# Expert stage: row loads wait for the group six back, filling rows sent in four lots

## The chip, the core and the metric

One Trainium2 chip, of which one core is used. The metric is device microseconds of one execution, the median of three runs. The core has five engines that run their own instruction streams and meet at semaphores: PE (matmul; its weight loads are the rows of PEld), DVE, ACT, POOL and SP. SP only issues transfers here. POOL issues the indirect transfers, in which every row of a tile goes to an address of its own.

## What is computed

The whole program is two transformer-like layers; the change touches only the last part of the second, a mixture of experts over 8 x 512 tokens of width 256 with 16 experts, each token going to its best two:

```
router_logits = sigmoid(x @ gate_w + gate_b)
expert_values, expert_indices = top_k(router_logits, k=2)
expert_values = expert_values / sum(expert_values)
hg = x @ experts_wg[e];  hu = x @ experts_wu[e]      # 256 -> 128, per expert
out_e = (silu(hg) * hu) @ experts_wd[e]              # 128 -> 256
return x + shared_mlp(x) + sum_k expert_values[k] * out_e[k]
```

## The kernel before

The stage ahead of this one writes a row for each (token, expert) pair into a scratch tensor in HBM, `rows_dram`, sorted by expert: 512 16-bit words of the token (a high and a low part of 256 values), the row of the result that it is for, and its gate value. Each expert has a region of its own there. The expert stage (`expert_stage`, from L1973) then works through 80 tiles of 128 rows: 64 full tiles, whose places and experts are known only at run time, and 16 last tiles, one for each expert, of which only a part is filled. So that a last tile can be read whole, 128 *filling rows* are scattered behind the rows of each expert (L2016), 16 indirect transfers by POOL; they point at spare rows of the result.

Four tiles make a group: `G=4`, `NG=20` groups, of which `NF=16` (groups 0 to 15) hold full tiles and 16 to 19 the last tiles. Each group goes through this pipeline:

- SP loads its four tiles into one of six buffers, `xt[:,g%XB]`, `XB=6` (L1997 to L1999). It first reads the address of each tile (L1998). For g >= 6 it first waits (L1996) on the semaphore of a scatter, and for g == 16 on all filling rows (L1995).
- PE transposes the four tiles, 16 transposes, "turn" (L2024 to L2029); ACT and DVE copy them out of PSUM (L2068, L2091).
- PE multiplies by the gate and up weights, 48 matmuls, `upward` (L2046). The expert of a full tile is a register value, so the address of its weights is computed by PE's sequencer in between. For groups 16 to 19 it is a constant.
- ACT takes silu (L2079), DVE multiplies (L2102), ACT and DVE split the product into two 16-bit parts (L2082, L2104).
- PE multiplies by the down weights, 12 matmuls, `downward` (L2054); ACT and DVE scale by the gate value into one of four output buffers, `yt[:,g%YB]`, `YB=4` (L2072, L2095).
- POOL scatters the four output tiles to `found_dram` (L2020), reading the target rows from the group's `xt` buffer. That is why an `xt` buffer is free only when its group is scattered. There are four scatter semaphores, `scattered[g%YB]`.

In PE's order the turn of group g+1 stands ahead of `upward(g)`, and `downward(g-1)` behind it. So PE runs turn(g+1), upward(g), downward(g-1), turn(g+2) and so on; a turn that waits holds up the matmuls of the groups before it. On ACT and DVE the order is: copy of the turned g+1, work on g, output of g-1.

POOL's order is: 16 transfers of filling rows, then the scatters of groups 0 to 19. When all scatters have landed (L2000) SP reads the results back in eight pieces, DVE adds the two results of a token and the base, and SP stores the output (L2001 to L2012).

Of the kernel before, what the change touches and what calls it, by code (L numbers as in the profile page):

```python
# [34 lines left out]
@contextmanager  # L35
def semaphores(nc, stage):

    taken=[]
    def take(name):
        taken.append(nc.alloc_semaphore(name=stage+name))  # L40
        return taken[-1]
    yield take
    nc.clear_and_free_semaphores(taken)
    nc.all_engine_barrier()
# [1928 lines left out]
def expert_stage(nc, XT, HT, ident, wall, tile_row, last_row, group_experts, pad, pad_row, rows_dram, found_dram, out):  # L1973

    NT=NB*T//P; REGION=NB*T+P; FULL=2*NT; MAXT=FULL+NE; ROW=D+2; I32=mybir.dt.int32
    base=HT[:,:,:,:].rearrange("p k b t -> p (k b t)").rearrange("p (j d) -> p j d",d=D)
    room=XT[:,:,:,:].rearrange("p k b t -> p (k b t)")
    with ExitStack() as c2:
        sb2=lambda n,s,d=F32: c2.enter_context(nc.sbuf_tensor("exp_"+n,s,d))
        sem2=c2.enter_context(semaphores(nc,"exp_"))  # L1980
        G=4; NG=MAXT//G; NF=FULL//G; NC=NT//G; XB=6; YB=4
        ps=lambda n,s,d=F32: c2.enter_context(nc.psum_tensor("exp_"+n,s,d))
        px=[ps(f"turned{i}",[P,2,4,P],F16) for i in range(2)]; ph=[ps(f"hg{i}",[P,512]) for i in range(2)]; pu=[ps(f"hu{i}",[P,512]) for i in range(2)]; pd=[ps(f"out{i}",[P,2,D]) for i in range(2)]
        identh=sb2("identh",[P,P],F16)
        xt=sb2("xt",[P,XB,G,ROW],I32); xT=sb2("xT",[P,2,G,4,P],F16); si=sb2("silu",[P,2,512]); tg=sb2("tg",[P,2,512]); hid=sb2("hid",[P,2,2,512],F16)
        ob=sb2("ob",[P,2,G,D])
        found=room[:,0:4*G*D].rearrange("p (u c j d) -> p u c j d",u=2,c=2,d=D); yt=room[:,4*G*D:(4+YB)*G*D].rearrange("p (u j d) -> p u j d",u=YB,d=D)
        idh=sem2("identh"); loaded=[sem2(f"loaded{i}") for i in range(XB)]; turned=sem2("turned"); xt_kept=[sem2(f"turned_kept{i}") for i in range(2)]; up_done=sem2("up_done"); silu=sem2("silu"); product=sem2("product"); hi=sem2("hi"); lo=sem2("lo"); down=sem2("down"); y_kept=[sem2(f"y_kept{i}") for i in range(2)]; scattered=[sem2(f"scattered{i}") for i in range(YB)]
        pads_sent=sem2("pads_sent"); back=[sem2(f"back{i}") for i in range(2)]; paired=sem2("paired"); summed=sem2("summed"); stored=[sem2(f"stored{i}") for i in range(2)]
        block=c2.enter_context(nc.Block())  # L1990
        def words(g,d): return xt[:,g%XB].bitcast(d)
        @block.sync
        def _(sp):
            for g in range(NG):
                if g==NF: sp.wait_ge(pads_sent,16*NE)  # L1995
                if g>=XB: sp.wait_ge(scattered[g%YB],16*G*((g-XB)//YB+1))  # L1996
                for i in range(G):  # L1997
                    r=sp.value_load(tile_row[g*G+i:g*G+i+1,0:1] if g<NF else last_row[0:1,(g-NF)*G+i:(g-NF)*G+i+1],min_val=0,max_val=NE*(REGION+P)-P)  # L1998
                    sp.dma_start(xt[:,g%XB,i],rows_dram[bass.ds(r,P),:]).then_inc(loaded[g%XB],16)  # L1999
            for i in range(YB): sp.wait_ge(scattered[i],16*MAXT//YB)  # L2000
            def store(m):  # L2001
                sp.wait_ge(summed,m+1)
                for b in range(NB):
                    sp.dma_start(out[b,m*G*C:(m+1)*G*C,:].rearrange("(j t) d -> t j d",t=C),ob[b*C:(b+1)*C,m%2]).then_inc(stored[m%2],16)  # L2004
            for m in range(NC):
                if m>=2: sp.wait_ge(paired,m-1)
                for c in range(2):
                    at=c*NB*T+m*G*P
                    sp.dma_start(found[:,m%2,c],found_dram[at:at+G*P,:].rearrange("(j q) d -> q j d",q=P)).then_inc(back[m%2],16)
                if m: store(m-1)  # L2010
            store(NC-1)
            for i in range(2): sp.wait_ge(stored[i],16*NB*NC//2)  # L2012
        @block.gpsimd
        def _(pool):
            for e in range(NE):
                nc.gpsimd.indirect_dma_start(rows_dram[:,:],bass.IndirectOffsetOnAxis(pad_row[:,e:e+1],0),pad[:,e,:],None).then_inc(pads_sent,16)  # L2016
            for g in range(NG):
                for i in range(G):
                    if i%2==0: pool.wait_ge(y_kept[i//2],g+1)
                    nc.gpsimd.indirect_dma_start(found_dram[:,:],bass.IndirectOffsetOnAxis(words(g,U32)[:,i,D:D+1],0),yt[:,g%YB,i],None).then_inc(scattered[g%YB],16)  # L2020
# [158 lines left out]
def build(nc, a, out):  # L2179

    with ExitStack() as ctx:
# [39 lines left out]
        pad=sb("pad_rows",[P,NE,D+2],mybir.dt.int32); pad_row=sb("pad_row",[P,NE],U32)  # L2221
        rnn_dispatch_stage(nc,XT,HT,a["L1_cond2_Wx"],a["L1_cond2_Wh"],a["L1_cond2_b"],h0T,*[a["L1_ffn_"+n] for n in ("gate_w","gate_b","shared_wg","shared_wu","shared_wd","experts_wg","experts_wu","experts_wd")],ident,wall,tile_row,last_row,group_experts,pad,pad_row,rows_dram)
        expert_stage(nc,XT,HT,ident,wall,tile_row,last_row,group_experts,pad,pad_row,rows_dram,found_dram,out)


# [36 lines left out]
```

## Time and profile before

| | us |
|---|---|
| median of three runs | 3835.32 (3834.57 to 3835.72) |
| the profiled execution | 3842.36 |
| its span, first to last instruction | 3840.4 |
| expert stage, first load issued to last scatter issued | 3565.1 to 3783.8 |
| reading back and adding | 3785.4 to 3840.4 |

All times of the rows are from the start of the span, in us. A row of a timeline is one instruction, or some of one kind run together: start, duration, engine, line, operation, what it writes and reads, and in brackets how long its engine was idle before it and what ended that. Indirect transfers show only the time that POOL takes to issue them. In the chain of waits a row "DMA x<-y" is the time from issue until the data had landed. The ends of matmuls are modelled.

### The profile page before, as it was taken

The numbers are of one execution on the slowest core, as the hardware profiler recorded it, in microseconds if no ns is written. First come the engines' busy times: TensorE is split into PE (matmuls) and PEld (weight loads), VectorE is DVE, ScalarE is ACT, GpSimd is POOL, SyncE is SP. The second block draws the span as 40 slices with busy tenths as digits, with TensorE's granted clock in tenths as the row PEclk, the third lists the DMA queues.
The fourth block names the chain that finished last, engine by engine and source line by source line (L and its number), as shares of the span: only waits on it lengthen the run. The fifth ranks groups of instructions, "written<-read, shape, count | busy, mean of one in ns | idle before, by whom it ended". The sixth has DMA issues, their size and how long they took to land. (4 is left out here: it accounts for less than half of the span.)

```text
span 3840.4 us, 143685 instructions
## 1 busy us (share of the span) xinstructions
PE 3163.6 (82%) x58952; PEld 2402.2 (63%) x58952; DVE 2258.7 (59%) x6772; ACT 1695.6 (44%) x5164; POOL 1211.7 (32%) x1528
## 2 busy tenths in 40 slices
PE   8677488988889888489985899999999889999571
PEld 5445188888888888445532566666666567777451
DVE  4667644444444444368865888889888845555232
ACT  2179333333333333257743555565555534444230
POOL 0032410000000000033310655565555544444332
PEclk9899755555555555589997999999999955555786
DMA  4011100000000000010001000000000010110336
GB/s 132 1 55 46 31 25 14 25 14 14 25 14 25 14 14 25 13 34 21 20 1 52 2 3 3 2 3 3 2 3 2 16 50 31 33 33 28 109 97 173
DMA packets 112984, 116.09 MB, mean 30 GB/s; under 512 B 55041, under 2 KB 96458, under 8 KB 112371
## 3 DMA queue, kind: packets, MB, share of 16 engines
q1 hardware_dynamic: 104674, 87.36, 8.0%
q0 software_dynamic: 7824, 21.46, 1.5%
q8 instruction: 403, 6.60, 0.7%
q14 instruction: 83, 0.67, 0.1%
HBM read 79.65 MB, written 29.13 MB: 28 GB/s over the span
## 5 line engine op out<-in xcount | busy, mean ns | idle before, releaser
L676 PE MATMUL banks<-hp,whp 128*128 128x8 f16 x24576 | 741.4, 168 | 118.3 <-DVE hp L743 118.3
L676 PEld LDWEIGHTS banks<-hp,whp 128*128 128x128 f16 x24576 | 697.7, 104 | 179.1 <-DVE hp L743 170.2
L709 ACT ACTIVATE ig<-banks 128x32 f32<-128x32 f32 x512 | 101.4, 198 | 576.8 <-PE banks L676 576.8
L738 DVE SCALAR_TENSOR_TENSOR carry<-ig 128x16 f32<-128x16 f32 x512 | 92.1, 180 | 425.4 <-ACT ig L709 425.4
L646 POOL COPY HT<-hist 128x128 f32 x64 | 21.3, 408 | 987.0 <-DVE hp L748 987.0
L1747 PE MATMUL rnn_banks<-rnn_hp,rnn_whp 128*128 128x8 f16 x6144 | 285.6, 171 | 41.1 <-ACT rnn_hp L1805 15.6
L1747 PEld LDWEIGHTS rnn_banks<-rnn_hp,rnn_whp 128*128 128x128 f16 x6144 | 247.8, 107 | 108.3 <-ACT rnn_hp L1805 76.6
L1088 ACT ACTIVATE att_PH<-att_stp 128x1024 f16<-128x1024 f32 (+3 forms) x258 | 183.4, 711 | 296.6 <-PE att_stp L888 296.6
L1147 POOL TENSOR_TENSOR att_QK<-att_rot,att_QK 128x512 f16<-128x512 f32 x133 | 187.4, 1409 | 244.1 <-ACT att_QK L1080 244.1
L654 PE MATMUL banks<-xs,wxp 128*128 128x64 f16 x3168 | 263.7, 241 | 0.0
L1007 DVE TENSOR_TENSOR att_PL<-att_P,att_PH 128x1024 f16<-128x1024 f32 (+3 forms) x257 | 236.0, 957 | 0.5 <-issue 0.2
L1899 DVE TENSOR_TENSOR rnn_hp<-rnn_hist,rnn_hp 128x16 f16<-128x16 f32 x512 | 97.9, 191 | 228.7 <-ACT rnn_hist L1806 214.6
L1805 ACT ACTIVATE rnn_hp<-rnn_banks 128x16 f16<-128x16 f32 x512 | 94.3, 184 | 280.5 <-PE rnn_banks L1747 278.4
L832 PE MATMUL att_pj<-att_hT,att_w 128*128 128x512 f16 x804 | 199.2, 384 | 17.2 <-POOL att_hT L1151 15.4
L1138 POOL TENSOR_TENSOR att_ab<-att_ab,att_rope 128x512 f32<-128x512 f32 x134 | 170.0, 1269 | 131.7 <-DVE att_ab L980 128.7
L990 DVE TENSOR_REDUCE att_mx<-att_sp 128x2 f32<-128x264 f32 (+3 forms) x263 | 209.9, 820 | 1.1 <-PE att_sp L862 1.1
L654 PEld LDWEIGHTS banks<-xs,wxp 128*128 128x128 f16 x3168 | 194.6, 126 | 0.0
L1142 POOL TENSOR_TENSOR att_rot<-att_ab 128x512 f32<-128x512 f32 x134 | 185.6, 1385 | 15.3 <-POOL att_ab L1138 1.0
L901 PE MATMUL att_acc<-att_V,att_PH 128*128 128x65 f16 (+1 forms) x3584 | 181.1, 193 | 3.4 <-DVE att_PL L1010 3.4
L1093 ACT ACTIVATE att_P<-att_stp 128x1024 f32<-128x1024 f32 (+3 forms) x258 | 180.4, 699 | 5.3 <-DVE att_PL L1007 5.3
L901 PE MATMUL att_acc<-att_V,att_PL 128*128 128x65 f16 x1792 | 175.8, 192 | 0.0
L743 DVE TENSOR_TENSOR hp<-og,tc 128x16 f16<-128x16 f32 x512 | 90.2, 176 | 144.8 <-ACT tc L715 144.8
(595 smaller groups left out, 7767.1 us busy)
## 6 DMA issues: line engine op xcount, KB each, us to landing
gen_w<-in_L_cond_W_dram SPq DMA_DIRECT2D x32, 512.0 KB
exp_xt<-expert_rows_scratch SPq DMA_DIRECT2D x80, 129.0 KB
edge_cb<-cols_scratch SPq DMA_DIRECT2D x16, 512.0 KB, 3.7
XT<-expert_found_scratch SPq DMA_DIRECT2D x16, 512.0 KB, 5.0
mod_xn<-in_x_dram SPq DMA_DIRECT2D x8, 512.0 KB
XT<-in_xT_dram SPq DMA_DIRECT2D x1, 4096.0 KB
out_dram<-exp_ob SPq DMA_DIRECT2D x64, 64.0 KB, 2.2
attw_st<-in_L_attn_w_qkvT_dram SPq DMA_DIRECT2D x6, 512.0 KB
```

What stands on the lines that cost most here:

```text
L654: last=nc.tensor.matmul(out, wxp[:,wpart,k,col:col+128], xs[:,st,xpart,k,steps], start=False,stop=False,skip_group_check=True)
L676: last=nc.tensor.matmul(out, whp[:,wpart,k,col:col+128], hp[:,k,hpart], start=False,stop=True,skip_group_check=True)
L832: last=nc.tensor.matmul(pj[:,:],c_.w_of(n)[:,wpart,k,col:col+P],h_of(n)[:,xpart,k,PM:PM+T],start=(i==0),stop=(i==5)); i+=1
L901: last=nc.tensor.matmul(out[:,0:wide],p[:,h,at:at+P],V[:,n%4,tt,part,h,0:wide],start=(tt==0 and a==0 and p is PH and part==0),stop=(tt==(R ...
L990: i=nc.vector.tensor_reduce(out=mx[:,:,qt:qt+1],in_=s_ps[:,:,at:at+w_],axis=X_AX,op=ALU.max); at+=w_
L1007: i=nc.vector.tensor_tensor(PL[:,:,at:at+w_],P32[:,t%2,:,0:w_],PH[:,:,at:at+w_],ALU.subtract)
L1088: nc.scalar.activation(PH[:,:,at:at+w_],st_ps[:,:,0:w_],ACT.Exp,scale=DH**-0.5)
L1093: i=nc.scalar.activation(P32[:,t%2,:,0:w_],st_ps[:,:,0:w_],ACT.Exp,scale=DH**-0.5)
L1138: nc.gpsimd.tensor_tensor(ab[:,1],ab[:,1],c_.tab[:,1],ALU.mult).then_inc(turned,1)
L1142: nc.gpsimd.tensor_tensor(rot_of(j),ab[:,0],ab[:,1],ALU.add).then_inc(summed,1)
L1147: nc.gpsimd.tensor_tensor(dst[:,1],rot_of(j),dst[:,0],ALU.subtract).then_inc(lo,1)
L1747: last=nc.tensor.matmul(pre(st,par)[:,u,j], whp[:,wpart,k,u*P:u*P+P], hp[:,k,hpart], start=False,stop=True,skip_group_check=True)
```

## The change

Two edits in `expert_stage`.

1. The wait ahead of the load of group g (g >= 6) names the semaphore of group g-6, whose buffer is taken. Before, it named the semaphore with the number g%4 with the count for g-6. In effect, group 6 waited for group 2, 7 for 3, 8 and 9 for nothing more, 10 for 6, 11 for 7, 14 for 10, 15 for 11, 18 for 14 and 19 for 15. After, group g waits for g-6, throughout.
2. The filling rows are sent in `PG=4` lots of four transfers, ahead of the scatters of groups 0, 1, 2 and 3. Each lot first waits until group g+1 is turned.

```
-        G=4; NG=MAXT//G; NF=FULL//G; NC=NT//G; XB=6; YB=4
+        G=4; PG=4; NG=MAXT//G; NF=FULL//G; NC=NT//G; XB=6; YB=4
...
                 if g==NF: sp.wait_ge(pads_sent,16*NE)
-                if g>=XB: sp.wait_ge(scattered[g%YB],16*G*((g-XB)//YB+1))
+                if g>=XB: sp.wait_ge(scattered[(g-XB)%YB],16*G*((g-XB)//YB+1))
...
         @block.gpsimd
         def _(pool):
-            for e in range(NE):
-                nc.gpsimd.indirect_dma_start(rows_dram[:,:],bass.IndirectOffsetOnAxis(pad_row[:,e:e+1],0),pad[:,e,:],None).then_inc(pads_sent,16)
             for g in range(NG):
+                if g<PG:
+                    pool.wait_ge(turned,2*(g+2))
+                    for e in range(g*NE//PG,(g+1)*NE//PG):
+                        nc.gpsimd.indirect_dma_start(rows_dram[:,:],bass.IndirectOffsetOnAxis(pad_row[:,e:e+1],0),pad[:,e,:],None).then_inc(pads_sent,16)
                 for i in range(G):
                     if i%2==0: pool.wait_ge(y_kept[i//2],g+1)
```

## Rows read from the trace of the kernel before

**Rows 1.** SP's own waits, 3560 to 3841: what, released by, total us, times, longest.
```profile
SPq L1998 <- DMA expert_found_scratch<-XT,exp_xt: 41.3, 4, 19.8
```

**Rows 2.** Waits of the engines, 3600 to 3790, same columns.
```profile
POOL expert_found_scratch L2020 <- ACT XT L2072: 102.1, 16, 16.1
...
PE exp_turned L2028 <- DMA exp_xt<-expert_rows_scratch: 41.7, 5, 11.5
```

**Rows 3.** Timeline of PE: turns of group 6 and of group 18.
```profile
3632.52 1.89 PE L2028 MATMUL exp_turned<-exp_identh,exp_xt 128*128 128x128 f16 x16 [10.46 <-DMA exp_xt<-expert_rows_scratch]
...
3753.39 1.89 PE L2028 MATMUL exp_turned<-exp_identh,exp_xt 128*128 128x128 f16 x16 [11.46 <-DMA exp_xt<-expert_rows_scratch]
```

**Rows 4.** Timeline of POOL: first and last filling transfer, then scatters.
```profile
3564.89 0.96 POOL L2016 DMA_INDIRECT expert_rows_scratch<-pad_rows,pad_row  x1 [9.00 <-POOLq L44]
...
3583.91 0.96 POOL L2016 DMA_INDIRECT expert_rows_scratch<-pad_rows,pad_row  x1 [0.30 <-issue]
3600.99 0.96 POOL L2020 DMA_INDIRECT expert_found_scratch<-XT,exp_xt  x1 [16.12 <-ACT XT L2072]
...
3622.56 0.96 POOL L2020 DMA_INDIRECT expert_found_scratch<-XT,exp_xt  x1 [0.30 <-issue]
...
3740.43 0.96 POOL L2020 DMA_INDIRECT expert_found_scratch<-XT,exp_xt  x1 [4.06 <-ACT XT L2072]
...
3761.52 0.96 POOL L2020 DMA_INDIRECT expert_found_scratch<-XT,exp_xt  x1 [11.24 <-ACT XT L2072]
...
3782.86 0.96 POOL L2020 DMA_INDIRECT expert_found_scratch<-XT,exp_xt  x1 [0.31 <-issue]
```

**Rows 5.** Timeline of DVE: L2102 of groups 1, 4, 9, 10, 12, 15, 17, 19.
```profile
3598.64 0.69 DVE L2102 TENSOR_TENSOR exp_tg<-exp_silu,exp_hu 128x512 f32<-128x512 f32 x1 [2.44 <-ACT exp_silu L2079]
...
3621.47 0.69 DVE L2102 TENSOR_TENSOR exp_tg<-exp_silu,exp_hu 128x512 f32<-128x512 f32 x1 [1.60 <-issue]
...
3679.82 0.69 DVE L2102 TENSOR_TENSOR exp_tg<-exp_silu,exp_hu 128x512 f32<-128x512 f32 x1 [4.12 <-ACT exp_silu L2079]
...
3688.80 0.69 DVE L2102 TENSOR_TENSOR exp_tg<-exp_silu,exp_hu 128x512 f32<-128x512 f32 x1 [5.52 <-ACT exp_silu L2079]
...
3706.44 0.69 DVE L2102 TENSOR_TENSOR exp_tg<-exp_silu,exp_hu 128x512 f32<-128x512 f32 x1 [5.36 <-ACT exp_silu L2079]
...
3738.08 0.69 DVE L2102 TENSOR_TENSOR exp_tg<-exp_silu,exp_hu 128x512 f32<-128x512 f32 x1 [5.37 <-ACT exp_silu L2079]
...
3759.16 0.69 DVE L2102 TENSOR_TENSOR exp_tg<-exp_silu,exp_hu 128x512 f32<-128x512 f32 x1 [3.15 <-ACT exp_silu L2079]
...
3769.51 0.69 DVE L2102 TENSOR_TENSOR exp_tg<-exp_silu,exp_hu 128x512 f32<-128x512 f32 x1 [0.19 <-ACT exp_silu L2079]
```

**Rows 6.** Busy time by stretch; last three columns: granted clock, DMA share, GB/s.
```profile
3564.90:3587.50 22.60, 6.48 (x51) 5.20 (x52) 0.69 (x1) 1.02 (x1) 15.40 (x16) 0.50 0.51 152
...
3632.50:3639.70 7.20, 7.18 (x76) 6.78 (x77) 1.25 (x2) 1.62 (x2) 0.00 (x0) 0.70 0.50 129
3639.70:3662.60 22.90, 21.63 (x231) 15.93 (x228) 8.39 (x16) 8.61 (x15) 10.46 (x11) 1.00 0.28 88
3680.40:3704.30 23.90, 21.59 (x230) 15.94 (x228) 7.71 (x15) 8.01 (x14) 11.10 (x12) 1.00 0.29 93
```

**Rows 7.** Timeline of SP: the loads in three stretches, merged.
```profile
3570.46 14.20 SPq L1999 DMA_DIRECT2D exp_xt<-expert_rows_scratch  x6
...
3588.58 13.94 SPq L1999 DMA_DIRECT2D exp_xt<-expert_rows_scratch  x13
...
3625.87 18.39 SPq L1999 DMA_DIRECT2D exp_xt<-expert_rows_scratch  x16
```

**Rows 8.** Chain of waits: start, us, what; a group's last scatter and last load landing.
```profile
3744.24 2.40 DMA expert_found_scratch<-XT,exp_xt
...
3751.17 2.17 DMA exp_xt<-expert_rows_scratch
```

**Rows 9.** DMA queues, 3605 to 3663: packets, MB, share of 16 engines.
```profile
q8 instruction: 5, 0.08, 0.7%
```

## The prediction

> **What bounds the kernel now.** The change touches only the expert stage, so the first thing to look for is who waits there. I read the waits of SP, then those of the engines, then the timelines of PE, POOL and DVE around them. SP stands still 41.3 us in 4 waits at L1998, each ended by the landing of a scatter [rows 1]. PE stands still 41.7 us in front of turns, each ended by the landing of a load [rows 2]. These are the same four stalls, one after the other: turn(6), turn(10), turn(14) and turn(18); the first is 10.46 us and the last 11.46 us [rows 3]. The reason is the semaphore: load(6) needs the buffer of group 0 but waits for group 2, load(10) needs 4 and waits for 6, and so on. The reader can follow the first: group 2's last scatter is issued at 3622.56 [rows 4] and lands about 2.4 later [rows 8], at 3625.0; SP's loads start at 3625.9 [rows 7], the fourth is issued some 4 us later and lands 2.2 after that [rows 8], and turn(6) starts at 3632.52. Group 0 was scattered 18 us earlier. Since PE takes its work in order, upward(5) and downward(4) are held too, though their data is there. So the cycle of four groups is bound by scatter, load, turn, and not by an engine.
>
> Between the stalls something else sets the pace: PE with its weight addresses. Three groups take 22.9 and 23.9 us on PE with PE busy for 21.6 of it [rows 6], 7.6 and 8.0 a group. DVE's L2102, which follows each `upward`, comes every 7.6 us in groups 1 to 4 ((3621.47-3598.64)/3) but every 8.9 in groups 9 to 12 ((3706.44-3679.82)/3) [rows 5].
>
> **Part 1, the wait.** Removed: the four stalls. Nothing is added; SP waits at the same place for an earlier event. What is late next? In steady work the scatter of group j starts 2.35 us after L2102 of group j+1 (3738.08 to 3740.43, [rows 4, 5]), takes 4 x 1.27 us (the step of POOL's indirect transfers, (3583.91-3564.89)/15 [rows 4]), and lands 2.4 after its last start: 8.6 us after L2102 of j+1. The loads of j+6 then need 4 x 1.15 (18.39/16, [rows 7]) and 2.2 to land, so they are there 15.4 us after L2102 of j+1. Turn(j+6) comes behind upward(j+4), thus three groups later, 23 us at 7.6 a group. That leaves 7 us of slack or more. The output buffers are not late either: the output of j+4 is written over four groups after j.
>
> So the new pace is that of PE, P. I don't know it better than the two stretches: 7.6 to 8.9. I take the middle, 8.2: the first stretch ends right at a stall and the other doesn't, and I can't say which of them a run without stalls is like. The stalled restart disappears as well (granted clock 0.70 in the 7.2 us after the stall, 1.00 in the stretches after it [rows 6]); that is already in P, since groups between the stalls run at 1.00.
>
> Now to the end. L2102 of group 15 comes at 3738.08; with pace P from group 1 it would come at 3598.64 + 14 P = 3713.4 for P = 8.2: 24.7 us earlier. The end of the stage is POOL: from the first scatter of group 14 (3740.43) to the last of group 19 (3782.86) it takes 42.4 us [rows 4], with the stall of turn(18) inside it (the 11.24 idle us ahead of 3761.52 and a smaller gap after). Without that stall POOL has work all the time, because the last four groups have constant weights and come about as fast as it can send (two groups in 10.35 us, 5.2 each, in L2102 from group 17 to 19 [rows 5], against its 5.1) and it is a group behind by then: 23 steps x 1.27 = 29.2 us. That is 13.2 us less. After it nothing changes: the read-back waits for the same landing. Sum of part 1: 24.7 + 13.2 = 37.9 us.
>
> **Part 2, the filling rows.** Sixteen transfers of 1.27 us are moved past POOL's first scatters; none is removed. What was at the place they leave: they ran from 3564.89 to 3584.87, ahead of the first scatter at 3600.99, for which POOL was waiting 16.12 us anyway [rows 4]. So POOL gains nothing there. But while they ran everything else was slow: six loads took 14.2 us (2.4 each) against 13 in 13.9 (1.07 each) once they were over [rows 7], and PE got through 51 matmuls in 22.6 us at clock 0.50 [rows 6]. If that is their doing, it goes. Bounds: with loads at 1.1 us from the start, the eighth load is issued at about 3573 and lands at 3575; turn(1) and upward(0) at low clock take some 7 us, so upward(0) ends near 3582 where it now ends just before 3591: at most 8.8 us gained. The other bound is zero: the first lot now waits for turn(1) and so falls on upward(0), with the same loads beside it. I take 2 us, near the lower end, since a quarter of the filling rows still falls there, and the slow steps could belong to the entry of the stage.
>
> At the place they go to: POOL does a lot (5.1 us) and a scatter (5.1) in turn, 10.1 us a group, slower than P. From the scatter of group 0 at 3601 the scatters of groups 1, 2 and 3 start at 3611, 3621 and 3631.4; the last of group 3 is issued by 3636.5. Group 4's output is ready at about 3598.64+4x8.2+2.4 = 3633.8, so POOL is late by 3 us there and in time from group 5. Who waits for that? The loads of 7, 8 and 9. The tightest is load(9): group 3 landed at 3637.6, four loads and landing 6.8, there at 3644.4. Turn(9) is six groups behind turn(3) (near 3599): 3648 at P = 8.2, 3644.8 at 7.6. It fits, barely, so the cost is 0 to 1 us, and it would be a few us if loads are slow beside POOL's transfers. The outputs of groups 0 to 3 have buffers of their own, and that of group 4 needs only the scatter of group 0. L1995 finds all filling rows landed long before group 16.
>
> The Trainium skill has a number on this (DMA: Bandwidth & Descriptors, section on latency and other measured facts): HBM access takes 0.2 us on average and 2 us at high load. By it a load lying among scatters and filling rows could land up to 2 us later than the 2.17 of rows 8, and turn(9) would stall for up to 2 us; an estimate from the page, and the sum would be 2 us smaller.
>
> **Sum.** 37.9 + 2 = 40 us less. The profiled execution took 3842.36 (span 3840.4 and 1.96 around it), 7.0 more than the median of the runs. I take the difference as it is: 3802.4 for a profiled one, 3795 for the median.
>
> **Rivals.**
>
> *The slower pace holds.* In groups 9 to 12 the period was 8.98 and then 8.82 (3688.80 to 3706.44 is twice 8.82) [rows 5], although PE's own rows allow 8.0. If a long run without stalls settles there, part 1 gives 3738.08 - (3598.64+14x8.87) = 15.3, plus 13.2, and 0 to 2 for part 2: 28 to 31 us, 3804 to 3807. For it: it is the longest stretch without a stall. Against it: two stretches of 7.6.
>
> *The faster pace holds and the start is freed.* P = 7.6 gives 33.0 + 13.2, and up to 8.8 more: 46 to 55 us, 3780 to 3789. The extra in the pace could be the reading of PE's instructions, of which five blocks fall in 58 us [rows 9], about one for each group. The Trainium skill says (Runtime: NRT & Kernel Launch, instruction fetch mechanics) that crossing into the next 16 KiB block is mostly hidden. By that rule the pace would be the 7.6 of PE's steps; the stretch at 8.87 speaks against it.
>
> *The filling rows take the place of the first stall.* If the loads crawl beside POOL as they did at 2.4 us, load(9) is there 5 us later, and the delay hits turn(7) to turn(9) as well. Price: up to the 10.5 of the first stall, giving 3805.
>
> *The change doesn't do what it says*: PE's turns wait on something else. Nothing in the rows points to it: all four long stalls are ended by that load. 3835.
>
> *Slower.* One mechanism: all sequencers step slowly while POOL's indirect transfers and SP's loads run side by side. At the start upward(0) took near twice its time. Until now scatters met loads only in bursts after a stall, when PE was idle or just starting; from now on they meet in every group, and POOL is busy without a break from 3601 to 3636. If PE's work took twice as long in those 36 us and for the 5 us of scatters of the twelve groups after, it would cost about 18 + 30 = 48 us and more, against 40 gained: 3843. It decides from the point where PE loses about 2.5 us a group. Against it: PE worked at full pace during the scatters of rows 6 (11 and 12 of them in the two stretches).
>
> **Chances.** Forecast, 3788 to 3801: 0.40. Slower pace, 3801 to 3810: 0.27. Fast, 3778 to 3788: 0.18. Filling rows stall, 3801 to 3812: 0.08. No difference, within 0.2% (7.7 us, about what can be told from no change): 0.02. Slower: 0.05. The range is 3782 to 3812; it leaves out the lower half of the fast case, the no-change case and the slower one.
>
> **What to look at afterwards.** Right on part 1: no row of PE with an idle of 9 to 11 us at L2028, SP's wait of 41.3 us moved to times when six groups are loaded ahead, L2102 of group 15 near 3711, POOL without a gap from the scatter of group 14 on, 29 us to its end. Right on part 2: lots of four at L2016 between the scatters, scatter of group 3 near 3631, first loads at 1.1 us. Wrong if turn(7) to turn(9) wait for loads, if L2102 comes every 8.9 us, or if PE shows gaps in `upward` beside the scatters.

## The result

| | us | against the kernel before |
|---|---|---|
| kernel before, median of 6 runs | 3834.83 (3831.91 to 3835.72) | |
| changed kernel, median of 6 runs | 3821.34 (3816.91 to 3823.66) | ratio 0.9965, 95% interval 0.9952 to 0.9977 |
| changed kernel, profiled execution | 3823.53, span 3821.6 | |

The change saves 13.5 us, a third of the 40 that were forecast; 3821 lies outside the range of 3782 to 3812.

The experiments fell on two kinds of surroundings, and no sentence below can be understood without this: in three sets of runs, the one of the result among them, the kernel before takes 3833 to 3841 us; in the three others 3807. Where the chip is on record, the sets of the first kind ran on chips 7 and 14, those of the second on 10 and 11. I call them chips of the first and of the second kind, though no run shows what differs. Every ratio is against the kernel before in the same set.

### The profile page after: what moved, and what is told of

The parts are those of the page before. It is cut to its first block and busy times, and to the rows that moved or that the text cites. A ratio compares the mean times of both kernels' runs of the same rounds, so it can differ in the third digit from the quotient of the medians.

```text
span 3821.6 us, 143685 instructions
## 1 busy us (share of the span) xinstructions
PE 3165.9 (83%) x58952; PEld 2401.0 (63%) x58952; DVE 2258.3 (59%) x6772; ACT 1694.0 (44%) x5164; POOL 1211.7 (32%) x1528
## 5 line engine op out<-in xcount | busy, mean ns | idle before, releaser
L1747 PEld LDWEIGHTS rnn_banks<-rnn_hp,rnn_whp 128*128 128x128 f16 x6144 | 248.3, 107 | 106.9 <-ACT rnn_hp L1805 75.8
```

What stands on the lines that cost most here:

```text
L1747: last=nc.tensor.matmul(pre(st,par)[:,u,j], whp[:,wpart,k,u*P:u*P+P], hp[:,k,hpart], start=False,stop=True,skip_group_check=True)
```

## The profile after

The stage begins where the stages before it let it, so I measure from SP's first load. The 80 loads as one merged row (SP's timeline), then DVE's L2104 (it was L2102) of groups 0, 1, 2, 3, 4, 5 and 15, answering [rows 5]:

```profile
3560.69 167.27 SPq L1999 DMA_DIRECT2D exp_xt<-expert_rows_scratch  x80
```

```profile
3579.29 0.69 DVE L2104 TENSOR_TENSOR exp_tg<-exp_silu,exp_hu 128x512 f32<-128x512 f32 x1 [6.16 <-ACT exp_silu L2081]
3584.99 0.69 DVE L2104 TENSOR_TENSOR exp_tg<-exp_silu,exp_hu 128x512 f32<-128x512 f32 x1 [0.71 <-ACT exp_silu L2081]
3599.46 0.69 DVE L2104 TENSOR_TENSOR exp_tg<-exp_silu,exp_hu 128x512 f32<-128x512 f32 x1 [11.01 <-ACT exp_silu L2081]
3605.96 0.69 DVE L2104 TENSOR_TENSOR exp_tg<-exp_silu,exp_hu 128x512 f32<-128x512 f32 x1 [3.04 <-issue]
3627.09 0.69 DVE L2104 TENSOR_TENSOR exp_tg<-exp_silu,exp_hu 128x512 f32<-128x512 f32 x1 [3.24 <-ACT exp_silu L2081]
3635.96 0.69 DVE L2104 TENSOR_TENSOR exp_tg<-exp_silu,exp_hu 128x512 f32<-128x512 f32 x1 [5.42 <-ACT exp_silu L2081]
...
3723.29 0.69 DVE L2104 TENSOR_TENSOR exp_tg<-exp_silu,exp_hu 128x512 f32<-128x512 f32 x1 [5.30 <-ACT exp_silu L2081]
```

Group 0 comes 18.6 us after the first load, where it came after 26.3. But group 2 comes 14.5 us after group 1, and group 4 comes 21.1 us after group 3. From group 5 to 15 each takes 8.73 us ((3723.29-3635.96)/10). The four waits of PE for loads [rows 2, 3] are gone: from 3575 to 3770 the waits of the engines hold no row of PE for a load. Two things are there instead. The first stands in PE's timeline (the bracket is idle time ahead of the row; "issue" means that nothing in the trace was waited for):

```profile
3592.65 0.62 PE L2030 MATMUL exp_turned<-exp_identh,exp_xt 128*128 128x128 f16 x7
3593.72 0.22 PE L2030 MATMUL exp_turned<-exp_identh,exp_xt 128*128 128x128 f16 x1 [0.46 <-issue]
...
3595.85 0.27 PE L2030 MATMUL exp_turned<-exp_identh,exp_xt 128*128 128x128 f16 x2 [1.18 <-issue]
...
3598.74 0.39 PE L2030 MATMUL exp_turned<-exp_identh,exp_xt 128*128 128x128 f16 x2 [0.46 <-issue]
...
3607.48 0.22 PE L2048 MATMUL exp_hu<-exp_xT,expert_weights 128*128 128x128 f16 x1 [0.39 <-issue]
...
3624.56 0.58 PE L2048 MATMUL exp_hu<-exp_xT,expert_weights 128*128 128x128 f16 x4 [1.12 <-issue]
```

PE steps from one instruction to the next in 0.7 or 1.4 us, where a matmul takes 0.2, though all its data is there. POOL's timeline of the same stretch, first and last transfer of two series, one of 8 without a break and one of 16 with one pause of 1.5 us (ahead of 3615.72), answering [rows 4]:

```profile
3587.35 0.96 POOL L2022 DMA_INDIRECT expert_found_scratch<-XT,exp_xt  x1 [9.91 <-ACT XT L2074]
...
3596.22 0.96 POOL L2019 DMA_INDIRECT expert_rows_scratch<-pad_rows,pad_row  x1 [0.30 <-issue]
3601.82 0.96 POOL L2022 DMA_INDIRECT expert_found_scratch<-XT,exp_xt  x1 [4.63 <-ACT XT L2074]
...
3622.06 0.96 POOL L2019 DMA_INDIRECT expert_rows_scratch<-pad_rows,pad_row  x1 [0.31 <-issue]
```

So the stops begin 5.3 to 5.9 us after the first transfer of a series and end 2.5 us after its last. In the steady groups a series has four transfers, and two stops are left of it, at the same place in each group:

```profile
3661.39 0.50 PE L2030 MATMUL exp_turned<-exp_identh,exp_xt 128*128 128x128 f16 x6 [0.56 <-issue]
3662.37 0.69 PE L2048 MATMUL exp_hg<-exp_xT,expert_weights 128*128 128x128 f16 x6 [0.48 <-issue]
```

The second thing is that PE's report of finished work arrives late. ACT's silu (L2081) waits for the semaphore that the last matmul of `upward` counts up. Group 2, PE's last row of `upward` and ACT's silu; then group 9, with the first and last scatter of the series between (timelines of PE, ACT and POOL; "remote" means that the profile can put the event down to no instruction):

```profile
3590.71 0.66 PE L2048 MATMUL exp_hu<-exp_xT,expert_weights 128*128 128x128 f16 x6
3598.83 0.60 ACT L2081 ACTIVATE exp_silu<-exp_hg 128x512 f32<-128x512 f32 x1 [10.85 <-remote]
...
3661.50 0.60 ACT L2081 ACTIVATE exp_silu<-exp_hg 128x512 f32<-128x512 f32 x1 [5.13 <-remote]
3664.48 0.96 POOL L2022 DMA_INDIRECT expert_found_scratch<-XT,exp_xt  x1 [4.00 <-ACT XT L2074]
3666.72 0.71 PE L2048 MATMUL exp_hu<-exp_xT,expert_weights 128*128 128x128 f16 x6
3668.28 0.96 POOL L2022 DMA_INDIRECT expert_found_scratch<-XT,exp_xt  x1 [0.30 <-issue]
3670.22 0.60 ACT L2081 ACTIVATE exp_silu<-exp_hg 128x512 f32<-128x512 f32 x1 [5.10 <-remote]
```

PE ends `upward(2)` at 3591.37, and ACT learns of it 7.5 us later, 2.6 us after the last transfer of the series of eight. PE ends `upward(9)` at 3667.43, and ACT starts 2.8 us later, 1.94 us after the last scatter. In groups 6 to 15 the lag behind PE is 2.5 to 2.9 us, and the distance from the last scatter is 1.9 to 2.0 us each time. This closes a loop that no engine's own speed sets: from silu(g) 3.0 us to the first scatter of g-1 (3661.50 to 3664.48), 3.8 us to the fourth, 1.9 us until the report of `upward(g+1)` gets through, together 8.7 us. With eight transfers in the series the same path takes 14.5 us (3584.36 to 3598.83), the long interval of group 2. Group 4 is the other case: PE itself ends `upward(4)` only at 3626.42, after slow steps from 3607.1 to 3624.6, and ACT starts 0.04 us later.

The end of the stage, in POOL's and PE's timelines:

```profile
3725.64 0.96 POOL L2022 DMA_INDIRECT expert_found_scratch<-XT,exp_xt  x1 [4.00 <-ACT XT L2074]
...
3740.82 0.96 POOL L2022 DMA_INDIRECT expert_found_scratch<-XT,exp_xt  x1 [5.34 <-ACT XT L2074]
...
3749.59 0.96 POOL L2022 DMA_INDIRECT expert_found_scratch<-XT,exp_xt  x1 [4.01 <-ACT XT L2074]
...
3763.54 0.96 POOL L2022 DMA_INDIRECT expert_found_scratch<-XT,exp_xt  x1 [0.30 <-issue]
```

```profile
3731.30 0.34 PE L2048 MATMUL exp_hg<-exp_xT,expert_weights 128*128 128x128 f16 x3 [1.02 <-issue]
...
3737.00 0.80 PE L2048 MATMUL exp_hu<-exp_xT,expert_weights 128*128 128x128 f16 x6 [0.92 <-issue]
```

The scatters of groups 14 and 15 stand back to back, and PE steps slowly from 3729.9 to 3737: POOL waits 5.34 us for the output of 16. It waits 4.01 us more for that of 17, and there PE is done in time; its report of `upward(18)` is 2.5 us late, 1.98 us behind the last scatter of 16. SP's last load is issued by 3728.0, so the loads are not needed for it.

## Where the time went

Microseconds between the same events in each trace; "forecast" is the prediction's own sum, applied to the trace before. "Wait alone" is the kernel of the next section.

| stretch | forecast | before | changed | wait alone | before, 2nd kind | changed, 2nd | wait alone, 2nd |
|---|---|---|---|---|---|---|---|
| first load to L2102 of group 1 | 31.5 | 33.5 | 24.3 | 31.9 | 24.4 | 22.8 | 24.4 |
| group 1 to 5 | 32.8 | 40.5 | 51.0 | 35.1 | 36.7 | 28.7 | 28.5 |
| group 5 to 15 | 82.0 | 98.9 | 87.3 | 84.5 | 88.1 | 75.8 | 72.5 |
| to the first scatter of group 14 | 2.4 | 2.4 | 2.4 | 2.4 | 2.4 | 2.4 | 2.4 |
| from there to the last scatter | 29.2 | 42.4 | 37.9 | 37.9 | 40.6 | 29.7 | 29.7 |
| to the end | 57.6 | 57.6 | 58.0 | 57.3 | 58.4 | 58.4 | 58.2 |
| sum | 235.5 | 275.3 | 260.9 | 249.0 | 250.6 | 217.8 | 215.7 |

Each column is one execution. That of before took 7.5 us more than the median of its runs and that of the changed kernel 2.2 more, but that of the wait alone (first kind) 6.9 less; so the 11.9 us between the last two overstate what the lots cost, and the timed runs decide.

## Experiments

### The wait alone

The kernel before with only the new condition of the loads; the filling rows stay at the start.

```
-                if g>=XB: sp.wait_ge(scattered[g%YB],16*G*((g-XB)//YB+1))
+                if g>=XB: sp.wait_ge(scattered[(g-XB)%YB],16*G*((g-XB)//YB+1))
```

> Only the wait is changed; the 16 filling transfers stay ahead of all scatters. Theory A: POOL's indirect transfers, sent without a break, slow every sequencer and hold back what PE reports, so the lots between the scatters cost about 18 us (groups 2 to 4) and freeing the start gives about 8 back. Then this kernel is about 10 us faster than the changed one: groups 1 to 15 at 8.7 us each, L2102 of group 15 at about 155 us after the first load is issued, median 3806 to 3814. Rival R: the lots cost nothing and the loads or PE's own work set the time of groups 2 to 4. Then this kernel is slower than the changed one by the 8 us of the start, about 3829.

> The kernel with the new wait alone once more, as the mark for the others of this call. If the kernel before takes some 3807 us here: 0.990 of it, as before. If it takes some 3835 us here: the theory of slow steps (unbroken series of indirect transfers make PE's and SP's instructions step at 0.7 us) expects group 0 late, 8.73 us a group from then on, no slow steps at the first groups, and 27 to 35 us under the kernel before, or 0.991 to 0.993; the rival (PE's own pace holds everywhere) expects 7.2 us a group and 0.980.

> The kernel with the new wait alone, beside the other of this call. Theory (the difference between the first chip and the later ones is in how PE and SP step beside GpSimd's indirect transfers, and not in the change): where the kernel before takes 3835 us, 8.7 us a group, group 0 at 26 us from the first load, and 27 to 35 us under the kernel before; where it takes 3807 us, 0.990 to 0.991 of it and 7.2 us a group. Rival (the forecast's own sum, pace held at 8.2 to 8.9 and the tail run through, was right for the wait and only the lots failed): 24 to 38 us under the kernel before at 3835 us.

Second kind: 3768.24 us and 3772.10, ratios 0.9899 (0.9884 to 0.9914) and 0.9910 (0.9894 to 0.9925), 34 to 39 us saved. First kind: 3814.08, ratio 0.9955 (0.9938 to 0.9971), 17 us (11 to 24) saved; its trace is 26 us under that of before, but of a single execution 6.9 us faster than the median, and I take the timed ones. L2102 of groups 3 and 4 there, then PE's two stops in one group:

```profile
3605.73 0.69 DVE L2102 TENSOR_TENSOR exp_tg<-exp_silu,exp_hu 128x512 f32<-128x512 f32 x1 [5.31 <-ACT exp_silu L2079]
3614.43 0.69 DVE L2102 TENSOR_TENSOR exp_tg<-exp_silu,exp_hu 128x512 f32<-128x512 f32 x1 [5.24 <-ACT exp_silu L2079]
```

```profile
3604.98 0.51 PE L2028 MATMUL exp_turned<-exp_identh,exp_xt 128*128 128x128 f16 x6 [0.50 <-issue]
3605.98 0.69 PE L2046 MATMUL exp_hg<-exp_xT,expert_weights 128*128 128x128 f16 x6 [0.49 <-issue]
```

8.7 us a group, and the tail of 37.9 of the changed kernel: both belong to the first kind and not to the lots. On the second kind it is 7.2 us a group and the tail is 29.7, half a microsecond off the forecast.

On the first kind the late report is in this trace too. PE ends `upward(2)` and `upward(3)` 7.1 and 7.9 us after the group before, yet ACT's silu comes after 8.9 and 8.8, each time 2.0 to 2.1 us after the last scatter of a series. On the second kind PE's last row of `upward(5)`, a scatter issued 0.39 us ahead of the silu, and the silu itself:

```profile
3605.89 0.66 PE L2046 MATMUL exp_hu<-exp_xT,expert_weights 128*128 128x128 f16 x6
3606.20 0.96 POOL L2020 DMA_INDIRECT expert_found_scratch<-XT,exp_xt  x1 [0.30 <-issue]
3606.59 0.60 ACT L2079 ACTIVATE exp_silu<-exp_hg 128x512 f32<-128x512 f32 x1 [3.53 <-PE exp_hu L2046]
```

ACT starts 0.04 us after PE, and so in every group of all twelve traces of the second kind, in the middle of series or not.

### Before and after again

> The changed kernel as it is, once more, beside the kernel before and the three other kernels of this call. Theory (the unbroken series of indirect transfers, one lot and one group's scatters back to back, let PE's and SP's instructions step at 0.7 us): the changed kernel is 10 to 16 us under the kernel before here too, its scale by the ratio 0.9965; its groups 2 and 4 take 14 and 21 us from one L2104 to the next, and groups 5 to 15 take 8.7 us each. Rival (the slow steps and the pace of 8.7 belong to the execution or the chip on which the profile was taken, since the kernel with the wait alone showed neither, at 7.2 us per group): the changed kernel comes within 5 us of the kernel with the wait alone, some 34 to 39 us under the kernel before, and its intervals are 7.2 us throughout.

> The kernel before, for its trace beside the others of this call. Theory (the unbroken series and the loop over PE's report are in the kernel itself): 8.87 us from one L2102 to the next between the stalls, four stalls of 10 to 11 us, SP's loads beside the filling rows at 2.4 us each, as in the first trace. Rival (they belong to the chip): 7.2 to 7.6 us between the stalls, loads at 1.2 us, and a time some 27 us shorter.

> The changed kernel beside these. If the kernel before takes some 3835 us here: 0.9965 of it, intervals of 14 and 21 us at groups 2 and 4, 8.73 us a group from 5 on. Theory (the slow steps make up the long intervals): these two intervals show in this execution too, at the same groups. Rival (they were an accident of one execution): at other groups or none. If it takes 3807 us: 0.991.

Second kind: changed kernel 3772.27, ratio 0.9913 (0.9899 to 0.9926), 33 us saved; the kernel before 3806.80 with its stalls in place, 7.2 us a group between them and first loads without slow steps. So each theory had half: the slow steps do belong to the surroundings, as the rival said, and where they are they come with the unbroken series. First kind once more: 3826.63, ratio 0.9963 (0.9950 to 0.9975), long intervals at groups 2, 3 and 4 (14.6, 13.1 and 14.4 us), again under POOL's series, here three of eight transfers. All three are late reports (7.6, 7.2 and 8.2 us behind PE).

On the second kind POOL's series is longer still, 40 transfers from 3574.4 to 3625.0 with no pause over 0.8 us; its timeline at two points, and PE's beside it, both of the changed kernel:

```profile
3589.90 0.96 POOL L2019 DMA_INDIRECT expert_rows_scratch<-pad_rows,pad_row  x1 [0.30 <-issue]
...
3619.89 0.96 POOL L2022 DMA_INDIRECT expert_found_scratch<-XT,exp_xt  x1 [0.30 <-issue]
```

```profile
3594.11 1.06 PE L2030 MATMUL exp_turned<-exp_identh,exp_xt 128*128 128x128 f16 x16
3595.07 0.66 PE L2048 MATMUL exp_hg<-exp_xT,expert_weights 128*128 128x128 f16 x6
...
3610.04 1.07 PE L2030 MATMUL exp_turned<-exp_identh,exp_xt 128*128 128x128 f16 x16 [1.46 <-DMA exp_xt<-expert_rows_scratch]
...
3619.05 1.07 PE L2030 MATMUL exp_turned<-exp_identh,exp_xt 128*128 128x128 f16 x16 [1.59 <-DMA exp_xt<-expert_rows_scratch]
```

No stop in `upward`; only turns 8 and 9 wait 1.5 us each for loads. That is the lots' own price there.

### The lots alone

The changed kernel with the old condition of the loads back.

> The changed kernel with the old condition of the loads back (they wait for the scatters two groups ago), so that only the move of the filling rows is left. Theory (the lots cost 18 us by slow steps, and their leaving the start frees some 8 us): 5 to 15 us slower than the kernel before, or 3812 to 3850 by where that stands; if the slow steps fall beside the stalls of the loads, which are there again, it comes within 5 us of the kernel before. Rival (lots cost nothing, the start is freed): 5 to 10 us faster than the kernel before. Second rival (the wait carried the whole gain and the lots lose it again through the loads alone): equal to the kernel before.

Second kind: 3811.76, ratio 1.0014 (1.0005 to 1.0023), 5 us slower than before. The stall of group 6 grows to 14.04 us from 7.51, since group 2's scatters, for which its load waits under the old condition, start 45.6 us after the first load instead of 41.1, and PE is there 1.8 us sooner. This kernel was not run on the first kind.

### What a lot costs: held time or transfers

The wait alone, and fills of an unused tile by POOL in place of the lots; 128x1024 first, then 128x1472, as long as a lot.

```
+                if g<4:
+                    pool.wait_ge(turned,2*(g+2))
+                    for e in range(4): nc.gpsimd.memset(busy[:,e],0.0).then_inc(idle,1)
+                    pool.wait_ge(idle,4*g+4)
```

> The kernel with the new wait alone, filling rows at the start as before, and in the place of each lot, ahead of the scatters of groups 0 to 3, four fills of an unused 128x1024 tile by GpSimd, about as long as the lot. It tells apart whether a lot costs because it occupies GpSimd's order or because it is a series of indirect transfers. Theory (indirect transfers slow the other engines' steps): GpSimd being late by 5 us for four groups costs nothing that lasts, since loads wait for scatters six groups back: within 3 us of the kernel with the wait alone (0.990 of the kernel before). Rival (occupation of GpSimd is the cost): 10 to 20 us more than that, as with the changed kernel.

> The kernel with the new wait alone and, ahead of the scatters of groups 0 to 3, four fills of an unused 128x1472 tile by GpSimd, sized to last 5.1 us, as long as a lot of four filling transfers; the shorter fills of 128x1024 held GpSimd 3.6 us each time and cost nothing. Theory (the time that GpSimd is held ahead of the scatters is what a lot costs): the loads of groups 7 to 9 come as late as in the changed kernel, two intervals of 8.5 to 9.5 us, and 3 to 5 us more than the wait alone. Rival (a lot costs by being indirect transfers): no interval over 7.5 us, the same as the wait alone.

> The kernel with the new wait alone and GpSimd's fills of 128x1472 tiles ahead of the scatters of groups 0 to 3, as long as the lots. If the kernel before takes some 3835 us here: theory (a lot costs by the unbroken series of indirect transfers, in which PE's instructions step at 0.7 us) expects no interval over 12 us in the first five groups after group 0, and a time within 4 us of the wait alone (0.9955); rival (GpSimd held is the cost, as at 3807 us) expects one or two intervals of 11 us or more at groups 6 to 9 and 4 to 8 us more than the wait alone. If it takes 3807 us: 0.992 again.

Second kind: short fills 3769.41, ratio 0.9906 (0.9891 to 0.9921), nothing lost; long fills 3775.95, ratio 0.9920 (0.9907 to 0.9934), 4 us over the wait alone of the same set, with one late load at turn(9):

```profile
3626.09 1.89 PE L2032 MATMUL exp_turned<-exp_identh,exp_xt 128*128 128x128 f16 x16 [3.72 <-DMA exp_xt<-expert_rows_scratch]
```

So there a lot costs because it holds POOL: scatters come late, and with them the loads six groups on. The intervals overlap, so it is the row and not the ratio that shows it. First kind: 3820.95, ratio 0.9951 (0.9934 to 0.9968), no more than the wait alone (0.9955), with no interval over 9.4 us in the first five groups; one of 13.9 follows at group 6. That is the interval by which the rival was to be known, but no load is late there: the fills had made the scatters of groups 3 and 4 stand back to back, a series of eight without any filling transfer, and PE's report of `upward(6)` came 7.0 us late behind it. Held time by itself does not make the 14 and 21 us of the changed kernel; the series of transfers does, whatever it carries. The ratio of the fills can't be told from that of the changed kernel of the same set (0.9963) either, so it is the trace and not the time that shows this.

### Smaller lots

`PG=8` and `PG=12` for `PG=4`.

> The changed kernel with its sixteen filling transfers in eight lots of two, ahead of the scatters of groups 0 to 7, where it has four lots of four. Theory (a lot costs because GpSimd then needs more than PE's 7.2 us for a group: 5.06 for four scatters and 5.06 for a lot of four make 10.1, so it falls 2.9 us further behind with each, and the load six groups on waits for it): with lots of two GpSimd needs 7.6 us a group, falls behind by 0.4 a group, and no load is late; 3 to 6 us faster than the changed kernel, 1 to 2 us faster than the one with the wait alone, because the start is freed (0.988 to 0.990 of the kernel before). Rival (any filling transfer between the scatters costs PE time): the same as the changed kernel, 0.991 to 0.993. If the kernel before shows 3835 us here and 8.9 us a group, the theory of slow steps has series of six instead of eight and more: 10 us faster than the changed kernel's 0.9965.

> The changed kernel with its filling transfers in twelve lots of one or two, ahead of the scatters of groups 0 to 11. Theory (held time on GpSimd): within 1.5 us of the kernel with eight lots of two, since there too no load is late. Rival (each lot costs something of its own, by number): 1 to 3 us slower than with eight lots.

> The changed kernel with eight lots of two. If the kernel before takes some 3835 us here: theory (series of eight or more let PE step slowly for as long as the part of the series beyond the first 5 us) expects series of six, slow steps of at most 3 us in each of eight groups, group 0 at 18 to 19 us from the first load, and 5 to 12 us less than the changed kernel; rival (each filling transfer costs its time wherever it stands) expects the changed kernel's time within 3 us. If it takes 3807 us: 0.990 again.

Second kind: 3769.29 and 3769.96, ratios 0.9904 (0.9889 to 0.9919) and 0.9900 (0.9885 to 0.9915), loads in time (one wait of 0.34 us in the first). From first load to end 213.4 and 213.8 us, the shortest of the kernels that do all the work: the freed start is kept. First kind: 3824.08, ratio 0.9955 (0.9939 to 0.9972), 2.6 us under the changed kernel of the same set, no difference that can be told. I expected 5 to 12. A series of six, POOL's first and last, and PE's stops:

```profile
3587.58 0.96 POOL L2022 DMA_INDIRECT expert_found_scratch<-XT,exp_xt  x1 [10.80 <-ACT XT L2074]
...
3593.91 0.96 POOL L2019 DMA_INDIRECT expert_rows_scratch<-pad_rows,pad_row  x1 [0.31 <-issue]
```

```profile
3593.34 0.27 PE L2030 MATMUL exp_turned<-exp_identh,exp_xt 128*128 128x128 f16 x2 [0.29 <-issue]
3594.78 0.27 PE L2030 MATMUL exp_turned<-exp_identh,exp_xt 128*128 128x128 f16 x2 [1.17 <-issue]
3596.24 0.83 PE L2030 MATMUL exp_turned<-exp_identh,exp_xt 128*128 128x128 f16 x12 [1.19 <-issue]
```

From 5.5 us after the first to 2.3 after the last, some 3 us of it. PE's report of `upward(2)` gets through 2.5 us after the last, so the loop takes 11.8 us with six transfers (the intervals are 11.8, 11.7, 14.1 and 11.7 us at groups 2, 3, 5 and 6), where it takes 8.7 with four: many short series cost what few long ones do.

### Filling rows by SP

The wait alone; SP writes the filling rows itself, with plain transfers, ahead of load(6).

> The wait is changed and the filling rows leave POOL altogether: they are 128 rows in a row behind each expert's rows, so SP writes them with 16 plain transfers, after the loads of groups 0 to 5. Theory A: no filling transfer is on POOL's queue, so neither the start is slow (L2102 of group 0 at about 19 us after the first load, against 26 before) nor groups 2 to 4; groups at 8.7 us, about 8 us faster than the kernel with the wait change alone, 3799 to 3806. Rival R2: it is the traffic of the filling rows and not POOL's queue that slows the others; then groups 1 to 4 show the same gaps of PE of 0.5 to 1.7 us each as in the changed kernel and the time is near 3815 to 3821.

Second kind: 3778.20, ratio 0.9920 (0.9907 to 0.9934), 8 to 10 us worse than the wait alone of the same set (6 in the traces). The loads of group 6 stand behind sixteen writes, which take SP 18.7 us to issue, and turn(6) waits for them:

```profile
3607.40 1.89 PE L2030 MATMUL exp_turned<-exp_identh,exp_xt 128*128 128x128 f16 x16 [7.96 <-DMA exp_xt<-expert_rows_scratch]
```

On the first kind this kernel was not run, so there theory A and R2 stay undecided.

### What sets the pace

The wait alone with the experts' numbers as constants in PE's program, and with every second scatter left out.

> The wait change alone, and the expert of every full tile is a constant instead of the register value, so PE's sequencer computes no weight addresses; the results use the wrong experts' weights. Theory B, the pace of 8.7 us a group is PE's own stepping: it falls to that of PE's matmuls, 76 x 0.06 = 4.6, or to POOL's 5.1. Theory A, the pace is a loop: PE's report of upward(g), 3.0 us to the first scatter of g-1, 3.8 to the fourth, 1.9 until PE's next report gets through: it stays at 8.7, or, if PE is done before the reports are held (they get through for some 2 us after the first scatter starts), it drops to about 5 to 6.

> The wait change alone, and two of the four scatters of each group are left out (half of the expert results are missing; the scratch tensor of results is filled beforehand, in a stage of its own at the start, which adds some tens of us). Theory A: the loop is shorter by two steps of 1.27, 3.0 + 1.3 + 1.9 = 6.2 us, so PE becomes the bound and a group takes about 7.6. Theory B: PE's stepping is unchanged, 8.7 us a group.

> The kernel with the new wait alone, in which PE takes its experts' numbers from constants instead of from registers, so that the products of most groups use other weights than the reference's. If the kernel before takes some 3835 us here: theory (the pace of 8.7 is a loop over GpSimd's four scatters and PE's report, 3.0+3.8+1.9 us, and not PE's addresses) expects 8 us a group or more; rival (PE's own instructions set it, as at 3807 us, where constants brought it from 7.2 to 5.4) expects 6 us or less.

Second kind: with constants 3744.95 us; L2101 of two groups in a row:

```profile
3641.12 0.69 DVE L2101 TENSOR_TENSOR exp_tg<-exp_silu,exp_hu 128x512 f32<-128x512 f32 x1 [1.42 <-ACT exp_silu L2078]
3646.01 0.69 DVE L2101 TENSOR_TENSOR exp_tg<-exp_silu,exp_hu 128x512 f32<-128x512 f32 x1 [1.42 <-ACT exp_silu L2078]
```

4.9 us, and some intervals of 6 where loads come late. With half the scatters the pace stays 7.1 (its total, 3806.22, holds a stage of its own that fills the result rows first). So PE's reading of the experts and its address arithmetic are the bound there, and not POOL. First kind: constants give 3807.94 us, in one execution. The intervals are uneven, from 3.5 to 13 us, since groups finished quickly line up their scatters, but no turn behind group 1 waits 0.3 us or more for a load, and their mean over groups 1 to 15 is 8.2 us: what the theory of the loop expected (8 or more) and not the rival's 6, though PE needs only 4.9 us a group.

### Scatters held back

The wait alone, and POOL holds the scatters of group g for `upward(g+2)`.

```
+                if g+2<NF: pool.wait_ge(up_done,g+3)
```

> The kernel with the new wait alone, and GpSimd holds the scatters of group g until PE has reported the upward products of group g+2, so that they never run beside PE's turns of group g+3. Theory for a chip on which the kernel before takes 3835 us (PE's instructions there stop for 0.6 us twice a group, at its turns, while scatters run, which makes 8.73 us a group of 7.2): the two stops move to other instructions of PE or go; where they go, 7.2 to 7.6 us a group. Rival: 8.7 us a group whatever the scatters' place. On a chip on which the kernel before takes 3807 us: PE's 7.2 us a group hold; the loads of groups 6 and later are released some 3 to 5 us later, which six buffers take, so within 3 us of the wait alone (0.990 to 0.991).

First kind: 3814.29, ratio 0.9948 (0.9931 to 0.9965), the same as the wait alone beside it. Steady groups take 8.2 us for 8.7. No report of groups 0 to 16 is late, since the scatters start behind it (ACT's silu again 0.04 us after PE), so what is left over 7.2 are PE's stops alone, some 1.0 us a group. They moved with the scatters, into `upward`:

```profile
3695.43 0.22 PE L2047 MATMUL exp_hg<-exp_xT,expert_weights 128*128 128x128 f16 x1 [0.52 <-issue]
3696.16 0.44 PE L2047 MATMUL exp_hg<-exp_xT,expert_weights 128*128 128x128 f16 x5 [0.51 <-issue]
```

What the pace gained, the end lost: the scatters of the last groups start later.

## Why the prediction was wrong

**The four stalls** were named rightly, and the new wait removes them, on both kinds.

**The pace** (P = 8.2, bounds 7.6 to 8.9). It came out at 8.73, within the bounds and near the rival at 8.87; over groups 5 to 15 that is 5.3 us of the shortfall. I took the stretch at 7.6 and the one at 8.9 for two samples of PE. They were not. L2102 of groups 2 and 3 of the kernel before, which stand inside the stretch at 7.6:

```profile
3607.61 0.69 DVE L2102 TENSOR_TENSOR exp_tg<-exp_silu,exp_hu 128x512 f32<-128x512 f32 x1 [5.50 <-ACT exp_silu L2079]
3616.41 0.69 DVE L2102 TENSOR_TENSOR exp_tg<-exp_silu,exp_hu 128x512 f32<-128x512 f32 x1 [5.34 <-ACT exp_silu L2079]
```

Its three intervals are 9.0, 8.8 and 5.1 us: two at the slow pace, and a short one that only makes up for the late report before it (2.8 us at group 3, 0.2 at group 4). So both stretches had the same pace, and what set it is not PE but the loop over POOL's scatters and PE's held report, of which the prediction has no term (PE's stops alone leave 8.2, as the scatters held back show).

**The tail** (13.2 us). It gave 4.5: 37.9 us against 29.2, the largest single error of part 1 at 8.7. The step that failed is that POOL has work all the time because PE's last groups are fast. POOL has two gaps instead, which are the whole error (5.0 and 3.7 us beyond its usual 0.3): PE is slow once, because the scatters of 14 and 15 run back to back, and its report is late once; the wait alone has the same 37.9. On the second kind the step holds to half a microsecond (29.7 in both kernels).

**The start** (2 us). 9.2 us by group 1, and 9.5 at the end of `upward(0)`, for which the bound of 8.8 stood: on the first kind the slow start was the filling transfers' doing, of which [rows 7] was the sign with loads of 2.4 us. On the second kind, where loads go at 1.1 to 1.3 us beside them, only 1.6 us are gained.

**The lots between the scatters** (0 to 1 us). This is the term that was most wrong. The prediction asked only whether a load comes late behind them; on the first kind none does. Groups 1 to 5 take 51.0 us, 18.2 over forecast, where the wait alone takes 35.1, because a lot lengthens the series to eight and more, and with it the hold on PE's reports and steps. This ate the start and the first stall's gain. The terms add up: 5.3 + 8.7 + 18.2 - 7.2 at the start + 0.5 at the end = 25.5 us of the forecast's 39.8, which leaves 14.3; the table has 275.3 - 260.9 = 14.4. Over the timed runs the lots matter less: 0.9965 and 0.9963 against 0.9955 for the wait alone, 3 to 4 us and within the intervals.

**The rival that came nearest** is the one I gave 0.05: all sequencers step slowly beside POOL's indirect transfers. Half of its mechanism was right and its price wrong: PE's steps are slow only from 4 to 6 us into a series, and it knew nothing of the late reports. A group costs 1.5 us more (8.7 for 7.2) and not 2.5, and the gain isn't turned around. What I held against it, that PE kept its pace during the scatters of [rows 6], was itself a sign: PE did three groups in 23.9 us, 8.0 each, while L2102 came 8.9 apart, so something behind PE set the pace.

On the second kind the same change saves 33 us and the wait alone 34 to 39; the sum of part 1, 37.9, was right there, with 3 to 4 us for the lots. Turn(9) waits 1.59 us for its load there, which the prediction put at "barely". The Trainium skill says (Runtime: NRT & Kernel Launch, instruction fetch mechanics) that crossing a block is mostly hidden. No run isolates that; the traces have 5 blocks between 3605 and 3663 on the second kind, at 7.2 us a group, and the same 5 on the first kind, at 8.9, so the number of blocks is not what tells the kinds apart.

```profile
q8 instruction: 5, 0.08, 0.6%
```

(kernel before, second kind, the answer to [rows 9].)

## What to carry to other kernels

A buffer's release must name the group that held it; a wrong semaphore costs whole stalls, and its removal is worth what the next pace allows. Before moving indirect transfers of POOL between other work, look in the trace for engines that wait for nothing while a series of them runs, and for engines that start long after the work they wait for has ended; count the transfers of each unbroken series rather than their sum. A pace is read from single intervals: a mean over a stretch that ends at a stall hid two slow intervals behind one short one here. Where an engine's own rows are closer together than those of the engine that follows it, the bound lies between the two.

## What was not expected of the hardware

On one kind of chip PE and SP step at 0.7 or 1.4 us an instruction from 4 to 6 us after the first to 2 or 3 us after the last of an unbroken series of POOL's indirect transfers (series of 4, 6, 8 and 16), and the semaphore that PE's last matmul counts up mostly arrives 1.9 to 2.2 us after the last of four transfers, 2.3 to 2.5 after the last of six and 2.5 to 2.7 after the last of eight, up to 8.2 us after the matmul. Reports made within 3 us of the first transfer sometimes get through earlier, so that a few groups come sooner (two of 7.2 us in the trace of the wait alone). On the other kind there is neither, in a series of 40.

The kernel before takes 3834.8 us in the set of the result and 3807 on the second kind, 28 us less. In the traces 24.7 us of the difference lie in this stage, in the stretches where the series run; the rest lies ahead of it and was not looked into. The way in which POOL's transfers hold the others, and what differs between the kinds, stays open: no run here looks inside it, and none tells whether the recording of the profile has a part in it.
